# A convolution, attention-score and normalization kernel: ScalarE issues the output stores on its own DMA queue

## What is computed

```
k   = einsum('ijk,imk->ijmk', hx, hy)          # per channel an outer product
y   = irfft2(rfft2(x) * rfft2(k) / 512)        # causal, the first 256 x 256
z   = y + x * bias[channel]
scores = einsum('bpsd,bptd->bpst', z, z) / 16
red    = sum(scores * weights[p], axis=t)      # one number for each row
y2     = z + red
out    = (y2 - mean) * rsqrt(var + 1e-5) * gamma + beta    # mean, var per channel
```

## Time and profile before

| | |
|---|---|
| median of 3 runs | 968.88 us (968.71 to 970.04) |
| the profiled execution | 968.82 us, its span 966.9 us |
| busy, share of the span | PE 98%, PEld 86%, DVE 78%, ACT 70%, POOL 69% |
| granted TensorE clock, mean | 0.992 |
| DMA | 235.90 MB, mean 244 GB/s, all on one queue apart from instruction fetches |
| chain that ended last | PE 95%, ACT 2%, DVE 1%, DMA 1% |

### The profile page before, as it was taken

How to read it: one execution, slowest core, us unless ns; L and a number is a source line. 1 busy time by engine, 2 the same in 40 slices (tenths; PEclk the granted TensorE clock), 3 DMA queues, 4 the chain that set the end, 5 groups by cost and what they waited for, 6 DMA issues and landing times.

```text
span 966.9 us, 18768 instructions
## 1 busy us (share of the span) xinstructions
PE 944.4 (98%) x5436; PEld 829.1 (86%) x5436; DVE 749.8 (78%) x2335; ACT 681.3 (70%) x1088; POOL 671.5 (69%) x518
## 2 busy tenths in 40 slices
PE   7999999999999999999999999999999999999993
PEld 5888888888888888888888888888888888888882
DVE  2678878878878878878878778788788788788785
ACT  2547777777777777777777777777767767767756
POOL 2767767767767777777777777777777777777750
PEclk9999999999999999999999999999999999999996
DMA  7765877878878887877778877877787787787634
GB/s 217 263 207 181 273 232 258 275 215 267 274 227 258 277 242 243 274 253 235 271 247 238 274 243 246 271 262 224 274 251 235 278 264 230 271 271 226 226 113 174
DMA packets 73294, 235.90 MB, mean 244 GB/s; under 512 B 7232, under 2 KB 24128, under 8 KB 65088
## 3 DMA queue, kind: packets, MB, share of 16 engines
q1 hardware_dynamic: 73280, 235.73, 75.8%
HBM read 168.40 MB, written 67.31 MB: 244 GB/s over the span
## 4 chain that ended last, share of the span: by engine, by line
PE 95%; ACT 2%; DVE 1%; DMA 1%; POOL 0%; issue 0%; ACTq 0%; DVEq 0%
PE ps_c L483 36%; PE ps_u L483 31%; PE ps_z L483 27%; PE ps_avg L483 1%; ACT out_sb L458 1%; DMA toep_whole<-filters_padded 1%; ACT z_sb L458 0%; DVE z_sb L678 0%; DMA par<-params_in 0%; POOL zl L391 0%; DVE products L700 0%; ACT zh L467 0%; DVE zl L689 0%; DMA filters_padded<-z_sb 0%; DVE z_sb L611 0%
## 5 line engine op out<-in xcount | busy, mean ns | idle before, releaser
L391 POOL TENSOR_TENSOR zl<-z_sb,zh 128x1024 fp32r<-128x1024 f32 x126 | 301.7, 2394 | 207.9 <-ACT zh L467 207.9
L700 DVE CUSTOM_DVE_ANT_0 products<-z_sb,ps_c 128x256 bf16<-128x256 f32 x508 | 183.6, 418 | 158.3 <-PE ps_c L483 158.3
L483 PE MATMUL ps_z<-uh,toep 128*128 128x512 f32 x768 | 270.8, 407 | 0.1
L437 ACT ACTIVATE uh<-ps_u 128x1024 fp32r<-128x1024 f32 x127 | 130.4, 1027 | 197.4 <-PE ps_u L483 197.4
L458 ACT ACTIVATE out_sb<-z_sb,shift,gain 128x256 f32<-128x256 f32 x496 | 257.1, 592 | 6.6
L483 PE MATMUL ps_u<-toep,xh 128*128 128x256 f32 x1016 | 240.0, 317 | 2.3 <-POOL toep L369 2.2
L483 PE MATMUL ps_c<-zh,wh 128*128 128x512 f32 x508 | 197.9, 389 | 1.2 <-DVE zl L689 0.7
L483 PE MATMUL ps_c<-zh,wl 128*128 128x512 f32 x508 | 198.1, 390 | 0.0
L483 PE MATMUL ps_c<-zl,wh 128*128 128x512 f32 x508 | 197.7, 389 | 0.0
L483 PE MATMUL ps_u<-toep_whole,xt_sb 128*128 128x128 f32 x1016 | 195.0, 273 | 0.0
L711 DVE BATCH_NORM_STATS2 stat<-z_sb 128x6 f32<-128x256 f32 x512 | 179.3, 413 | 0.0
(11 more groups left out here) (63 smaller groups left out, 924.9 us busy)
## 6 DMA issues: line engine op xcount, KB each, us to landing
xt_sb<-xt_in SPq DMA_DIRECT2D x64, 1024.0 KB, 9.3
x_sb<-x_in SPq DMA_DIRECT2D x128, 512.0 KB, 7.2
out<-out_sb SPq DMA_DIRECT2D x124, 512.0 KB, 3.5
w_sb<-wt_in SPq DMA_DIRECT2D x64, 256.0 KB, 6.7
toep_whole<-filters_padded SPq DMA_DIRECT2D x64, 256.0 KB, 6.5
out<-z_sb SPq DMA_DIRECT2D x4, 512.0 KB, 3.0
par<-params_in SPq DMA_DIRECT2D x1, 224.0 KB, 4.6
par<-params_in SPq DMA_DIRECT2D x1, 194.0 KB, 2.6
```

Source lines behind the costliest of these rows:

```text
L391: nc.gpsimd.tensor_tensor(zl[:, zs.slot(2)], z_sb[:, r, h], zh[:, zs.slot(2)].bitcast(F32), ALU.subtract)\
L437: nc.scalar.activation(uh[:, us.slot(2)], u_bank(us)[:, :, :, :], ACT.Copy)\
L483: return nc.tensor.matmul(o, a, b, start=start, stop=stop)
L700: last = nc.vector.tensor_tensor_reduce(products[:, cs.slot(2), k, b], z_sb[:, r, h, k, b], bank[:, k, b], 1.0 / math.sqrt(SIDE), 0.0, ALU ...
```

## The change

The stores are issued by ScalarE. In a step, ScalarE issues the store of the pair that it has just normalized, behind `zh` and behind a wait for its own `norm_done`. The stores of the last two pairs stand at ScalarE's end, behind the waits for `last_done` and `last_done_act`. SP's stage has the four loads alone, with their waits unchanged; its last steps end with the last load. It still waits for `stored` at the very end. Buffers, semaphores and the order of everything else stay.

```diff
-LOAD_AHEAD = 4
-LAG_STORE = LOAD_AHEAD + LAG_NORM + 1
...
             def stage(st):
 
-                done = st.trail(LAG_STORE)
-                if active(done):
-                    m, h = done.channel(), done.half()
-                    normed = z_sb[:, done.ring(XR), h] if ending(done, 4) else out_sb[:, h]
-                    if ending(done, 2):
-                        sp.wait_ge(last_done, done.number() - (PAIRS - 2) + 1)
-                        sp.wait_ge(last_done_act, done.number() - (PAIRS - 2) + 1)
-                    else:
-                        wait(sp, norm_done, done, 1)
-                    sp.dma_start(out[m, :, h, :, :, :].rearrange("p k b w -> p (k b w)"),
-                                 normed.rearrange("p k b w -> p (k b w)"))\
-                        .then_inc(stored[h], 16)
-
                 ts = st.trail(LAG_LOAD_T)
...
-            run_steps(sp, PAIRS, 2 * UNROLL, LAG_STORE, stage)
+            run_steps(sp, PAIRS, 2 * UNROLL, LAG_LOAD_X, stage)
...
         def _(act):
+
+            def store(done, normed):
+
+                nc.scalar.dma_start(out[done.channel(), :, done.half(), :, :, :].rearrange("p k b w -> p (k b w)"),
+                                    normed.rearrange("p k b w -> p (k b w)"))\
+                    .then_inc(stored[done.half()], 16)
...
                     nc.scalar.activation(zh[:, zs.slot(2)], z_sb[:, r, h],
                                          ACT.Copy).then_inc(zh_ready, 1)
 
+                if active(no) and not ending(no, 2):
+                    wait(act, norm_done, no, 1)
+                    store(no, z_sb[:, no.ring(XR), no.half()] if ending(no, 4) else out_sb[:, no.half()])
+
             run_steps(act, PAIRS, 2 * UNROLL, LAG_NORM, stage)
...
                 nc.scalar.activation(rows, rows, ACT.Identity, bias=shift[:, r, g:g + 1],
                                      scale=gain[:, r]).then_inc(last_done_act, 1)
+            for i in range(PAIRS - 2, PAIRS):
+                done = Step(0, i)
+                act.wait_ge(last_done, i - (PAIRS - 2) + 1)
+                act.wait_ge(last_done_act, i - (PAIRS - 2) + 1)
+                store(done, z_sb[:, done.ring(XR), done.half()])
```

## The result

| | before | with the change |
|---|---|---|
| median | 969.2 us (968.56 to 970.46, 20 runs) | 971.25 us (970.1 to 971.98, 20 runs) |
| profiled execution, its span | 968.82 us, 966.9 us | 970.28 us, 968.4 us |
| ratio of the times | | 1.0016, 95% interval 1.0009 to 1.0022 |

The change costs 0.16% of the time, 1.5 us. The predicted 970.3 us lies beside the profiled execution and 0.95 us under the median. By the bound of the prediction, 0.2%, it is no change; the interval says that it is slower by a little. Ten of the 20 runs before were at the upper one and eleven of the 20 with the change, so that one median falls into the gap between the levels and the other into the upper level. The means, 969.37 and 971.03 us, are 1.66 us apart.

The account below looks back on a forecast made before the run. The prediction took TensorE to bound the middle and ScalarE's normalizations, then the last stores, the end. It summed 0 in the middle, 0 at the start and +1.5 us at the end onto 968.82 for 970.3 us, range 968.9 to 972.3.

Parts of the forecast that it names:

- TensorE sets the middle, nothing is gained there: From 78.56 to 907.16 us: TensorE is busy for all 828.60 us, so quicker engines or queues gain 0.
- the one step that the prediction named: In the middle: without SP's wait for norm_done, loads go up to one step (7.2 us) earlier, gaining 0.
- The issue in the middle costs 0: Behind `zh` in each step: some 0.5 us of ScalarE time, hidden by its wait before `uh`; 118 or so issues cost 0.
- shorter by 0.1 to 0.5 us a step: In the middle, a sign of being right: ScalarE's wait before `uh` shrinks by 0.1 to 0.5 us a step.
- Only a ScalarE that is late by 3.7 us in a step stops TensorE: In the middle: the two covers, about 1.4 and 2.3 us, add to 3.7 us of lateness before TensorE stops.
- the room behind `zl`: In the middle, the second cover: `zl` ends 2.3 us before the first matmul that reads it starts.
- rival 2: Everywhere: ScalarE's queue stalls and TensorE waits, 1087 us at 4.7 us a step, or `out_sb` isn't free; 3 in 100 for both.
- Three stores at the end, 0.51 us each: In front of the fourth group of final activations: 0.10 drain, 0.02 release, 0.39 issue with restart each, together +1.5 us.
- D: At the end: the fourth activation group's half and its store, forecast to leave 1.5 us late and no more.
- E and F: The last two stores, behind the last two activations: their later issues cost nothing more, as the DMA engines are busy.
- Rival 1: At the end: ScalarE's issue costs 0.57 to 0.83 us like `w_sb` on SP, giving 971.0 to 971.8 us; 22 in 100.
- Roughly twice: In the middle: a store on its own queue row shares with loads, landing after roughly twice 3.5 us; sum still 970.3.

Follow-up runs that it names:

- 4 parts: The change with the last six stores back on SP and each store of pairs 0 to 121 cut into 4 DMAs on ScalarE: 969.79 us, ratio 0.9997.
- 6 parts: The change with the last six stores back on SP and each store of pairs 0 to 121 cut into 6 DMAs on ScalarE: 1046.5 us, ratio 1.0801.
- with 8: The change with the last six stores back on SP and each store of pairs 0 to 121 cut into 8 DMAs on ScalarE: 1210.2 us, ratio 1.2455.
- three waits: The kernel before, with ScalarE only waiting for norm_done behind pairs 122, 123 and 124 while SP issues the stores: 970.38 us, ratio 1.0004.
- last six stores on SP: The change, with the stores of pairs 122 to 127 given back to SP and the others still on ScalarE: 969.62 us, ratio 0.9998.
- three stores on ScalarE: The kernel before, with only the stores of pairs 122, 123 and 124 moved to ScalarE: 971.42 us, ratio 1.0015.

## Why the prediction was right, and where it wasn't

- **The number.** Right in the difference, 1.5 us, by the mechanism named. That 970.3 is also what the profiled execution took is partly luck: the sum starts from an execution at the lower level, and the one profiled with the change was at the lower level too. Eleven of the 20 runs were not.
- **TensorE sets the middle, nothing is gained there.** Right: 828.60 us busy before and after. SP's loads did go earlier, which nobody was waiting for: at the median by 2.1 us (`w_sb`), 2.4 (`xt_sb`, `x_sb`) and 13.6 (`toep_whole`), the last more than the one step that the prediction named.
- **The issue in the middle costs 0.** Right in its result, and for more than the reason given: the sum allowed 0.5 us of lost ScalarE time in front of `uh`, and the trace shows 0.00 in one kind of step and 0.04 in the other, as the issue runs beside `zh`. The sign "shorter by 0.1 to 0.5 us a step" did not come.
- **Only a ScalarE that is late by 3.7 us in a step stops TensorE.** Wrong, and it is the step that an experiment refuted. The wait before `uh` and the room behind `zl` were added as if each step had both anew. The second is there once: a lateness carried into the next step has used it. Taking ScalarE's own time in each step, the runs agree. From the start of `zh` to that of `xh` it is 0.97 us before, 2.27 with 4 parts, 3.34 with 6 and 4.27 with 8 (without the steps with the pause), that is 1.30, 2.37 and 3.30 more. The step grew by 0, 0.66 and 1.57. So what ScalarE can give is 1.7 us a step. That is a little less than all its idle time, (828.60 - 610.84) us in 828.60 / 7.22 = 115 steps, 1.9 us a step: the waits for VectorE's `z_sb` are part of that, and nearly all of them stay (48.5 of 52.5 us with 6 parts). The price of rival 2 rested on the 3.7; the rival wouldn't have come true with either.
- **Three stores at the end, 0.51 us each.** Right to 0.01 us: 0.52, D 1.53 us later. Both parts of the price, taken from other rows (the overlap of two activations, SP's issue for ScalarE's), were measured apart: 0.10 + 0.02 against 0.13, 0.39 against 0.39.
- **E and F are hidden behind D.** Right: 4 us at 393 GB/s behind D, as before. One sign was off: ScalarE's last activation was to end at about 963.6 and ends at 964.17. D's own issue stands in front of the last two activations, and the sum had left that 0.5 us out. It costs nothing, as E and F are not wanted so early.
- **Rival 1, an issue as long as those of `w_sb`.** It didn't come: 0.34 us at the end. The argument against it, that long issues stand behind other DMAs, fits the profile with the change: SP's `w_sb` issues fell from a median of 0.572 us to 0.333.

```profile
L272 SPq DMA_DIRECT2D w_sb<-wt_in x64: 327/333/467, 2.6 to 901.2; - x64
```

- **The store among the loads.** `out_sb` stores now land 5.6 us after their issue at the median, for 3.5, 1.6 times as long, and the longest took 9.6, less than the 12.2 us there are. "Roughly twice" was the estimate from the Trainium skill's turns between queue rows (DMA: Bandwidth & Descriptors, Queues, rings and completion order); the 1.6 is what sharing would give and doesn't prove it.

```profile
out<-out_sb ACTq DMA_DIRECT2D x124, 512.0 KB, 5.6
```

## What to carry to other kernels

In this kernel a DMA issued by a computing engine is free where that engine waits for others anyway, and it takes next to none of the engine's own time where it stands behind a long instruction. It costs its full drain and issue, here 0.52 us, where the engine's own chain is the end of the kernel. So count the issues on the last chain, not in the loop: three of 128 made the whole difference. And when asking how much a hidden engine can take, use its idle time a step, without the waits that stay (here 1.7 of 1.9 us), since the room further down the chain is spent only once. Where a change adds many instructions to a loop, look at the first instruction behind the branch too.

## What the runs showed that was not expected

**Two levels of the time.** The 20 runs before lie in two heaps, ten from 968.56 to 968.88 and ten from 969.52 to 970.46; those with the change nine from 970.1 to 970.9 and eleven from 971.21 to 971.98. Within each heap the change costs about 1.6 us (means 968.73 and 970.40; 970.00 and 971.54). The traces of the upper heap show where it comes from. From 20 to 30 us, in the kernel before (lower heap) and in the run with three waits (upper):

```profile
20.00:30.00 10.00, 8.50 (x60) 7.62 (x61) 3.68 (x3) 4.10 (x6) 7.53 (x6) 1.00 0.96 321
```
```profile
20.00:30.00 10.00, 8.23 (x48) 7.74 (x49) 1.97 (x2) 4.43 (x7) 6.93 (x6) 0.83 0.90 319
```

The granted clock is 1.00 in one and 0.83 in the other, so part of that stretch ran at the 1.2 GHz level: 48 matmuls instead of 60. All ten traces with a time of 966 to 973 us divide in this way: 1.00 in four (before, the change, last six stores on SP, 4 parts), with the last but one `shift` at 952.1 to 952.4 us, and 0.83 in six, with it at 953.3 to 954.2.

Ahead of that stretch the 28 warming products end at 19.12 us in the first (12.46 + 6.66) and at 18.76 in the second (12.10 + 6.66), and TensorE then waits for the first Toeplitz tile, for 2.25 us and for 2.95. But a longer pause is not what sets the two apart. The run with three stores on ScalarE has a shorter one than the kernel before, and the lower clock:

```profile
20.84 0.78 PE L490 MATMUL ps_u<-toep,xh 128*128 128x256 f32 x2 [2.18 <-POOL toep L369]
```
```profile
20.00:30.00 10.00, 9.02 (x51) 8.14 (x52) 2.63 (x3) 3.57 (x5) 7.02 (x6) 0.83 0.99 339
```

What decides it stays open. It is a chance of 1.1 to 1.3 us in every run, nearly as large as the effect studied.

**Several issues one behind another.** In the loop, from one issue to the next lie 0.48 us where nothing holds them ((3.66 - 0.32) / 7 for the eight at 608.49), 0.32 us of it the issue and the rest two register steps. But the register work is not what makes eight issues long. In the steps written out ahead of the loop there is none between the issues, and eight take as long, as each is then recorded with 0.44 us:

```profile
88.64 3.62 ACTq L403 DMA_DIRECT2D out<-out_sb  x8
```
